# An attention and mixture-of-experts kernel: down's product ahead of gate and up, and later turns, ranks and factors

## What is computed

```python
x = _layernorm(x + attention(x, Wq, Wk, Wv, Wo))           # window of 257 keys
probs = softmax(x @ kernel_router_DE)                      # D = 128, E = 8
weights, indices = top_k(probs, 2)
norm_weights = softmax(weights)
# of each token, for its two experts only (the reference computes all 8 and weights them):
fuse = _silu(x @ kernel_gating_EDF[e]) * (x @ kernel_up_EDF[e])      # F = 256
out += norm_weight * (fuse @ kernel_down_EFD[e])
x = _layernorm(x + out)
```

## Time and profile before

| | |
|---|---|
| runs (3) | 570.12, 575.82, 578.64 us; median 575.82 |
| profiled execution | 575.41 us, span from the first to the last instruction 573.8 |
| busy, share of the span | PE 483.0 us (84%), DVE 363.3 (63%), ACT 301.1 (52%), POOL 241.3 (42%) |
| granted clock of PE, mean | 0.924 |
| chain that ended last | PE 57%, DVE 17%, issue 10%, DMA 6% |
| costliest groups | L1328 DVE maxima 149.1 us, L1056 ACT exponentials 152.6, L790 PE values 90.7 |
| costliest of the units | L982 PE 47.6 us, L962 41.0, L963 36.5, L964 36.4 |

### The profile page before, as it was taken

One profiled execution on the slowest core, in us unless ns is written; L12 is line 12 of the kernel. 1 busy time (PEld: TensorE's weight loads), 2 busy tenths in 40 slices (PEclk: granted clock), 3 DMA queues, 4 the chain that ended last, 5 costly groups with the idle time before them and its releaser, 6 DMA issues.

```text
span 573.8 us, 12084 instructions
## 1 busy us (share of the span) xinstructions
PE 483.0 (84%) x3865; PEld 296.8 (52%) x3865; DVE 363.3 (63%) x825; ACT 301.1 (52%) x516; POOL 241.3 (42%) x329
## 2 busy tenths in 40 slices
PE   4399899899999999999998988977978899999700
PEld 3264345445454454445454444456867788888500
DVE  1366567778676496668688677652354645677784
ACT  2125455566556455466566466732575555555462
POOL 2131051752532232232746763007701727754772
PEclk9999798999999797799999799967998999999955
DMA  6343116126207225215205130111421445542362
GB/s 164 58 75 72 29 48 149 29 49 148 40 12 174 40 66 121 34 43 121 53 18 83 54 88 21 39 46 47 133 79 54 138 141 159 135 124 71 91 168 59
DMA packets 83948, 46.93 MB, mean 82 GB/s; under 512 B 40496, under 2 KB 79408, under 8 KB 83120
## 3 DMA queue, kind: packets, MB, share of 16 engines
q1 hardware_dynamic: 65216, 31.04, 24.4%
q0 software_dynamic: 4096, 8.40, 5.4%
q10 hardware_dynamic: 14576, 6.72, 4.3%
HBM read 26.47 MB, written 19.40 MB: 80 GB/s over the span
## 4 chain that ended last, share of the span: by engine, by line
PE 57%; DVE 17%; issue 10%; DMA 6%; SPq 3%; POOL 3%; ACT 3%; ACTq 0%; POOLq 0%; DVEq 0%
PE pV L790 12%; DVE mp L1328 7%; PE pX L982 6%; PE pX L962 5%; PE pX L715 5%; PE pX L964 4%; PE pX L963 4%; DMA xt<-xT 3%; DVE rden L1375 3%; PE pX L754 3%; PE pV L973 3%; PE pM L809 2%; PE pX L766 2%; PE pX L745 2%; SPq L435 2%
## 5 line engine op out<-in xcount | busy, mean ns | idle before, releaser
L1328 DVE TENSOR_REDUCE mp<-pX 128x4 f32<-128x1024 f32 (+4 forms) x128 | 149.1, 1187 | 84.4 <-PE pX L719 68.2
L1056 ACT ACTIVATE probs<-pX 128x1024 f32<-128x1024 f32 x152 | 152.6, 1023 | 91.3 <-PE pX L745 75.9
L790 PE MATMUL pV<-probs,vx 128*32 128x512 f32 (+1 forms) x736 | 90.7, 591 | 0.0
L647 POOL DMA_INDIRECT xs<-xr,slot x64 | 63.0, 985 | 44.6 <-DVE ends L1248 26.2
L659 POOL DMA_INDIRECT probs<-ys,source x64 | 64.0, 1001 | 38.1 <-issue 35.4
L715 PE MATMUL pX<-kx,q 48*128 48x512 f32 (+4 forms) x256 | 61.4, 479 | 9.4 <-DMA q<-q_scr 9.4
L754 PE MATMUL pX<-q,kx 50*128 50x512 f32 x248 | 63.0, 505 | 2.5 <-DVE mp L1328 2.0
L1421 DVE TENSOR_TENSOR probs<-probs,pX 128x512 f32<-128x512 f32 x44 | 30.3, 688 | 43.0 <-ACT probs L1118 43.0
L715 PEld LDWEIGHTS pX<-kx,q 48*128 48x128 f32 x256 | 26.2, 203 | 47.7 <-issue 36.1
L962 PE MATMUL pX<-we,qh 128*128 x88 | 41.0, 466 | 11.6 <-issue 9.5
L982 PE MATMUL pX<-we,probs 128*128 x352 | 47.6, 279 | 0.7 <-ACT vx L1130 0.7
(11 more groups left out here) (151 smaller groups left out, 832.5 us busy)
## 6 DMA issues: line engine op xcount, KB each, us to landing
q<-q_scr SPq DMA_DIRECT2D x46, 128.0 KB, 4.3
xt<-xs SPq DMA_DIRECT2D x88, 64.0 KB
ys<-vx ACTq DMA_DIRECT2D x44, 128.0 KB, 1.9
xt<-xT SPq DMA_DIRECT2D x8, 512.0 KB, 5.9
q_scr<-qh SPq DMA_DIRECT2D x32, 64.0 KB
q<-stage SPq DMA_DIRECT2D x128, 2.0 KB
xr<-x SPq DMA_DIRECT2D x8, 256.0 KB, 6.4
raw<-wgu SPq DMA_DIRECT2D x4, 512.0 KB, 5.7
```

Source lines behind the costliest of these rows:

```text
L647: pool.indirect_dma_start(xs[ph][:, :], bass.IndirectOffsetOnAxis(ap=slot[:, t, k:k + 1], axis=0), tile(t), None, bounds_check=ROWS - 1, o ...
L790: mm = pe.matmul(pV[row:row + 32, cols], vx[:, chunk, pr, :], src[:, pr, cols], start=n == 0, stop=True, skip_group_check=True)
L1056: act.activation(dst, src[:], ACT.Exp).then_inc(exp_done, 1)
L1328: dve.tensor_reduce(mp[:, t % 2, 0, :, i, :], src[:, :, 0:2 * n].rearrange("p r (c v k) -> p r v c k", v=NV, k=32), AX.XY, ALU.max).then_i ...
```

## The change

Seven edits, all of order or of grouping:

- On PE `down(k - 2)` stands ahead of `gate_up(k)` and `turn_hidden(k - 1)`; on ACT `rows_made(k - 2)` stands ahead of `silu(k)` and `hidden_out(k - 1)`.
- `MOE_STEPS`: steps NT + 2 to NT + 5, which turn tiles 28 to 31, stand in units 4 and 5, two in each, where they stood in units 3 to 6; each later step is one unit earlier.
- `RANK_AT`: the two last groups (tiles 24 to 27 and 28 to 31) are ranked one step later, which is the same unit as before; their place operations run one unit earlier.
- On DVE the seeds of the layer norm stand ahead of the place operations of the same step.
- The tables of the second and third part and POOL's `sort_rows` of tiles 24 to 31 are one unit earlier (13, not 14).
- `COMBINE_AT`: a part's first tile is combined 5 units behind its last unit, not 6.
- `SETS`: 20 tiles, then three times 4; before 16, then four times 4.

```diff
-SETS = [(0, TPS)] + [(t, t + 4) for t in range(TPS, NT, 4)]
+SETS = [(0, 20), (20, 24), (24, 28), (28, 32)]
...
-        RANK_AT[s_ + 1 + 3 * last_] = m_
+        RANK_AT[s_ + 1 + 4 * last_] = m_
...
-RANK_AT[8 * (NT // RT_TILES) + 12] = len(RANKED) - 1
+RANK_AT[8 * (NT // RT_TILES) + 13] = len(RANKED) - 1
...
-            COMBINE_AT.append(max([LAST_UNIT[part_of(t)] + 6] + [n + 1 for n in COMBINE_AT[-1:]]))
-        MOE_STEPS = {k: NT + i for i, k in enumerate((0, 1, 3, 4, 5, 6, 7, 8, 9, 10, 11, 12, 13, 14))}
+            COMBINE_AT.append(max([LAST_UNIT[part_of(t)] + 5] + [n + 1 for n in COMBINE_AT[-1:]]))
+        MOE_STEPS = {0: [NT], 1: [NT + 1], 4: [NT + 2, NT + 3], 5: [NT + 4, NT + 5]}
+        MOE_STEPS.update({k: [NT + k] for k in range(6, 14)})
...
                 if k + 1 < NU:
                     turn_rows(k + 1)
+                if k >= 2:
+                    down(k - 2)
                 if k:
                     gate_up(k)
                     turn_hidden(k - 1)
-                if k >= 2:
-                    down(k - 2)
...
                 if k + 1 < NU:
                     round_rows(k + 1)
+                if k >= 2:
+                    rows_made(k - 2)
                 silu(k)
                 if k:
                     hidden_out(k - 1)
-                if k >= 2:
-                    rows_made(k - 2)
```

More of the change, by code:

```diff
@@ L440, in attention_moe @@
         ZEROS_AT = (19, 26)
-        TABLE_AT = (14, 18)
+        TABLE_AT = (13, 18)
         COMBINE_AT = []
         for t in range(NT):
-            COMBINE_AT.append(max([LAST_UNIT[part_of(t)] + 6] + [n + 1 for n in COMBINE_AT[-1:]]))
-        MOE_STEPS = {k: NT + i for i, k in enumerate((0, 1, 3, 4, 5, 6, 7, 8, 9, 10, 11, 12, 13, 14))}
+            COMBINE_AT.append(max([LAST_UNIT[part_of(t)] + 5] + [n + 1 for n in COMBINE_AT[-1:]]))
+        MOE_STEPS = {0: [NT], 1: [NT + 1], 4: [NT + 2, NT + 3], 5: [NT + 4, NT + 5]}
+        MOE_STEPS.update({k: [NT + k] for k in range(6, 14)})
         block = ctx.enter_context(nc.Block())
@@ L681, in _ @@
             for k in range(NU):
-                if k in MOE_STEPS:
-                    step(MOE_STEPS[k])
+                for s in MOE_STEPS.get(k, ()):
+                    step(s)
                 if 2 <= k < 10:
                     sort_rows(14 + k)
-                if 14 <= k < 18:
-                    sort_rows(2 * k - 4)
-                    sort_rows(2 * k - 3)
+                if 13 <= k < 17:
+                    sort_rows(2 * k - 2)
+                    sort_rows(2 * k - 1)
             for t in range(NT):
@@ L1149, in _ @@
                     hidden_out(k - 1)
-                if k >= 2:
-                    rows_made(k - 2)
-                if k and k in MOE_STEPS:
-                    routing_exps(MOE_STEPS[k])
+                    for s in MOE_STEPS.get(k, ()):
+                        routing_exps(s)
             hidden_out(NU - 1)
@@ L1351, in step @@
                     dve.bn_aggr(mv[:, ((t - 1) // 4) % 2, (t - 1) % 4, :], st6[:, (t - 1) % 4, :]).then_inc(mv_done, 1)
[L1352 to L1357, removed]
                 g = ln_group(s)
@@ L1367, in step @@
                                       ALU.mult, ALU.add).then_inc(ln_seed, 1)
+                if s in SLOT_AT:
+                    for n in range(SL_OPS):
+                        slot_op(SLOT_AT[s], n)
+                for n in range(*TABLE_0.get(s, (0, 0))):
+                    if s < 30:
+                        table_op(0, n)
                 for n in range(*ops[0]):
@@ L1464, in _ @@
                 if k == 0:
-                    step(MOE_STEPS[k])
+                    step(NT)
                 if k + 1 < NU:
@@ L1468, in _ @@
                 hidden(k)
-                if k and k in MOE_STEPS:
-                    step(MOE_STEPS[k])
+                if k:
+                    for s in MOE_STEPS.get(k, ()):
+                        step(s)
                 for ph in range(1, NPH):
```

## The result

The changed kernel takes 620.45 us (median of 5 runs, 618.01 to 637.37), the kernel before 571.93 (5 runs, 570.12 to 578.64): ratio 1.083, 95% interval 1.076 to 1.090, so it is 8% slower, where 622 was forecast. Some executions of a kernel are some per cent longer at a lower granted clock; the ratios in this document leave them out, so a ratio can differ a little from that of the medians. The profiled execution of the changed kernel is one of its longer ones: 629.82 us, span 628.2, with granted clock 0.901 on average against 0.924, and 4.3 us of it were lost in attention, which the change leaves alone (the first gate/up product starts at 379.99, before at 375.72).

A forecast was written before the change was run, and what follows sets the result against it. PE bounds the expert stage. Starts: unit 5 404.65, plus 38 periods (182.4) and 0.9, unit 43 587.9; plus 3.0, VectorE 24.9, end 4.6: 620.4; plus 1.6 gives 622 us, 8-in-10 range 588 to 645.

The forecast's parts named there:

- What bounds it: Expert stage: PE's matrix work per unit is 1.40 + 0.44 + 0.89 + 0.25 = 2.98 us of a 3.23 period.
- The wait for hidT: In front of down: PE is free at +0.92, ScalarE's copy ends at +1.50, a stall of at least 0.58 us.
- The loads behind the wait: Before gate/up: the loads no longer run under matrix work, so it starts 1.66 + 0.4 us after the copy's end.
- The period: Each steady unit: 1.26 + 1.50 + 1.66 + 0.4 = 4.8 us (4.4 to 5.3), against 3.23.
- Walk through the first units: Gate/up starts: unit 2 at 388.5, 3 at 393.3, 4 at 399.6, 5 at 404.65; double turns cost about 1.5 and 0.25.
- the first case: Expert stage: PE stalls for the hidT copy at full clock, 622 us (608 to 638); chance 0.57.
- the second case: Expert stage: same stall, with the clock falling in part; half the units at about 6.6 us gives 656; chance 0.22.
- third case: In front of down: the loads run during the stall, period 3.75 to 3.9, 588 us; chance 0.13.
- fourth case: In front of down: the hidT copy hides under turn_rows, period stays 3.23, 10.9 us gained, 564.5 us; chance 0.08.
- The tail: After unit 43's hidden product: VectorE's 13 tiles and four sets take 24.9 us, then 4.6 to the span's end, 620.4.
- Gains of the other edits: Units 3, 12 and 35: removed waits, half-clock losses and earlier rows bring 10.9 us if the copy isn't waited for.
- no correction: Whole run: the profiled execution stands 0.4 us below the median of the runs, so the forecast was not adjusted.

The follow-up runs named there:

- experiment 4: Changed kernel with down and rows_made back behind gate/up and silu, and the next unit's two register loads right behind gate/up: 555.71 us, ratio 0.972.
- Experiment 3: Changed kernel with the two register loads of unit k+1 moved right behind gate_up(k): 584.43 us, ratio 1.026.
- experiment 5: Changed kernel with a third register load per unit, the second expert's number loaded twice: 683.17 us, ratio 1.193.
- experiment 12: Changed kernel with early loads, parts 16, 8, 8, single turns, down between gate/up and turn_hidden, rows_made between silu and hidden_out: 557.28 us, ratio 0.971.
- experiment 2: Kernel before with only down and rows_made moved ahead: 628.42 us, ratio 1.105.
- experiment 1: Changed kernel with down and rows_made back behind gate/up and silu, all other edits kept: 575.73 us, ratio 1.007.
- experiment 6: Kernel before with only the two register loads of the next unit moved right behind gate/up: 564.13 us, ratio 0.972.
- experiment 9: Changed kernel with down behind, early loads, parts 16, 8, 8, one turn step per unit: 678.25 us, ratio 0.980, where the kernel before took 690.28.

## Why the prediction was right, point by point

- **What bounds it.** Right. PE's work in a unit is 2.98 by the sum and 2.96 in experiment 4, where nothing else shows. Two of its terms are off and offset each other: six products take 1.49 up to the first turn by the earlier trace rows (499.89 to 501.38), not 1.40, and in experiment 4 the turns of the incoming rows cost 0.14 from start to start, not 0.25. The sum for the new period doesn't use this total.
- **The wait for hidT.** Right. The copy ends at +1.50, as taken from the earlier trace rows; PE's wait in front of L983 is 0.59, where 0.58 stood in the sum. That these agree so closely is luck: 0.58 ran from +0.92 to the copy's end, and 0.59 runs from the modelled end of the turns (+1.04) to down's start (+1.64).
- **The loads behind the wait.** Right, and shown by experiments 3 and 5: moving two loads takes 1.0 us off a unit, and one more adds 0.65. From the copy's end (544.51) to gate/up (546.55) are 2.04, where 1.66 + 0.4 stood in the sum. The value 0.4 was a choice between 0 and 0.89, and came out; down's four register operations, at 544.5 to 544.9 ahead of the first load, are what it stood for.
- **The period.** 4.88 on average against 4.8. Over the 38 units, 185.27 us against 182.4 + 0.9, that is 2.0 us. The 0.9 for the function tables was an estimate, and no run prices it alone.
- **Walk through the first units.** From the first gate/up, predicted and measured: unit 2 12.8 and 12.9, unit 3 17.6 and 17.7, unit 4 23.9 and 24.5, unit 5 28.9 and 29.9. The step that was mis-sized is the price of the double turns, taken as 1.5 + 0.25. Against a period of 4.86, unit 4 costs 1.93 more (6.79) and unit 5 0.51 (5.37), in all 2.4.
- **Clock.** It stayed at 1.00 from 410 to 590, so the first case came and not the second. The share of PE came to 72% by the busy time of the profile, not the 62% that the sum of starts gave, since modelled ends make busy times longer. Experiment 5 shows that the chance given to the second case was no waste: with one load more, 20 of 37 units ran at the lower clock. The prediction had no row that could tell one from the other, so the first case coming alone was in part luck.
- **Loads during the stall (third case).** It fell. The prediction drew on the Trainium skill, page "Advanced Engine Details and Errata", section "Sequencer and Instruction Queues", for it. What the page says is about engine instructions, and the wait here stands on a register operation, the one ahead of down's first product. The trace shows it to hold PE's program: that operation ran at 544.5, when the copy was done, and the loads at 545.1 and 545.7. Experiment 3 confirms it.
- **The copy not waited for (fourth case).** It fell with the 0.59, and experiment 12 shows the order in which it would have held.
- **The tail.** From unit 43 to the end 33.05 against 32.5: 13 tiles and four sets on VectorE with no wait for a gather. POOL waited 35.99 in front of tile 16, and 5.34 in front of tile 28 for unit 43's rows. These landed at 603.8, 8.7 behind the start of unit 43, where 9.1 stood in the prediction (597 - 587.9).
- **Gains of the other edits.** The walk counted them mainly as waits that vanish under a longer period, and there they were worth 5.7 us (experiment 2 against the changed kernel). In the fourth case the prediction gave them and the earlier rows 10.9 in all. With down behind they bring 2.8, so that case would have ended at about 573 and not 564.5: the pairs cost more than 1.75 (units 4 and 5 together take 14.77 us in experiment 1, 9.04 before), and the chain of gathers gives nothing for work saved behind unit 35.
- **The sum.** 0.9 in the first units, 2.0 in 38 periods, 0.6 in the tail and 4.3 in attention are the 7.8 us by which the profiled span (628.2) is above the forecast one (620.4). The median of the runs, 620.45, lies 1.5 below the forecast. Its run wasn't profiled; if its stage took the same 248.2, its attention was 5.1 shorter than the 375.72 that the forecast took over from the profile before, which hides 3.5 that the stage is longer than forecast. So the mechanism is right to some 7% of the loss (50.1 us in the stage, 46.6 forecast), and that 622 came out to 0.3% is luck. The same holds for "no correction": with five runs the kernel before has a median of 571.93, and its profiled execution stands 3.5 above it, not 0.4 below.

## What to carry to other kernels

Before moving a product, look at what its operand's copy waits for and what lies in between: here 0.25 us of work stood between a turn and the reader of its copy, and with the six products of gate/up in that place (experiment 12) down can stand ahead of the turns at no cost. A register load behind a wait is on the path, 0.65 us each here, so load the registers of the next unit right behind the longest group of products of this one; moving two loads made the kernel before 2 to 3% faster (experiment 6). When a chain of gathers with no gap leads to the end, only what comes before its first gather counts.

## What the runs showed of the hardware

- A register load costs PE 0.65 us, one after the other, when nothing covers it (experiment 5), though its own record is only 0.30 long.
- A wait on a register operation of PE holds the loads that follow it in the program: they ran at 545.1 and 545.7, behind the 544.51 that the wait was for.
- The granted clock stayed at 1.00 from 410 to 590 us of the changed kernel, with waits of 0.59 and 0.75 us in a unit of 4.80. In experiment 5, with one load more in each unit, 20 of 37 units ran in part or whole at the lower clock, which cost 1.46 us in a unit of 5.49.
- On one of four chips the same kernel before took 690 us and not 572 to 577, and the profile of experiment 9 from that chip has gaps of up to 19.82 us on PE that nothing in it releases, while POOL's transfers ran on. The cause is open.
- The releaser named before gate/up (VectorE's xl) was wrong in 28 of the 29 rows that have it; only in front of unit 0 was it the one waited for. Where two things end within a few tenths, the order of the program decides, and an experiment that moves one of them.
